# Clipped relative attention on one core: 64-row turns placed beside the scores, 64-column projections placed beside the values, and some copies moved between engines

## The reference

```python
q, k, v = split_heads(x @ Wq.T), split_heads(x @ Wk.T), split_heads(x @ Wv.T)   # 16 heads of 64
sim = einsum('bid,bjd->bij', q, k) * scale
idx = clip(r[None, :] - r[:, None], -16, 16) + 16
sim = sim + einsum('btd,tsd->bts', q, rel_k_table[idx]) * scale
attn = softmax(sim)
out = einsum('bij,bjd->bid', attn, v) + einsum('bts,tsd->btd', attn, rel_v_table[idx])
out = merge_heads(out) @ Wo.T + bo
```

## Time and profile before

| | |
|---|---|
| median of 3 runs | 2304.55 us (2299.51 to 2312.35) |
| profiled execution, own time | 2308.97 us |
| its span | 2307.3 us |
| TensorE busy / weight loads | 2030.2 us (88%) / 1226.8 us |
| VectorE, ScalarE, GpSimd busy | 1536.3, 1136.8, 746.6 us |
| mean granted TensorE clock | 0.955 |
| the stage that is changed | scores from 1605.1 to 2155.0 us of the span |

### The profile page before, as it was taken

One profiled execution on the slowest core, in us unless ns is written; L12 is line 12 of the kernel. 1 busy time (PEld: TensorE's weight loads), 2 busy tenths in 40 slices (PEclk: granted clock), 3 DMA queues, 4 the chain that ended last, 5 costly groups with the idle time before them and its releaser, 6 DMA issues.

```text
span 2307.3 us, 40672 instructions
## 1 busy us (share of the span) xinstructions
PE 2030.2 (88%) x15704; PEld 1226.8 (53%) x15704; DVE 1536.3 (67%) x3079; ACT 1136.8 (49%) x1854; POOL 746.6 (32%) x1057
## 2 busy tenths in 40 slices
PE   5886789988868989998998898998999999999888
PEld 2342466666644455445564344445666666666546
DVE  5685678888678777755556774024877777777663
ACT  2575456656614454563332566223664655646442
POOL 4544434333037847441002331002223232232133
PEclk7998899999979999999998999999999999999999
DMA  4430111111323524202002320001664564645252
GB/s 139 127 100 2 29 29 29 33 24 29 97 86 118 152 67 141 70 16 102 1 1 64 106 71 2 31 1 56 182 184 147 157 184 132 185 148 157 80 112 55
DMA packets 183975, 198.87 MB, mean 86 GB/s; under 512 B 55922, under 2 KB 152486, under 8 KB 179302
## 3 DMA queue, kind: packets, MB, share of 16 engines
q1 hardware_dynamic: 183782, 196.27, 28.9%
HBM read 93.53 MB, written 92.08 MB: 80 GB/s over the span
## 4 chain that ended last, share of the span: by engine, by line
PE 34%; DVE 10%; ACT 4%; DMA 3%; issue 2%; SPq 1%; POOL 1%; DVEq 0%; ACTq 0%; POOLq 0%
PE PS L2097 5%; DVE AR L2411 4%; PE PS L1950 3%; PE PS L2326 3%; PE PS L2333 2%; PE PS L1937 2%; PE PS L1940 2%; DMA RA<-ZP 2%; PE PS L2295 2%; PE PS L2348 2%; PE PS L2675 1%; ACT AR L2491 1%; DVE PS L2408 1%; PE PS L597 1%; PE PS L2365 1%
## 5 line engine op out<-in xcount | busy, mean ns | idle before, releaser
L2491 ACT ACTIVATE AR<-PS,AR 128x512 f32<-128x512 f32 x256 | 173.6, 686 | 181.1 <-DVE AR L2411 181.0
L1275 ACT ACTIVATE AR<-PS 128x1024 f32<-128x1024 f32 x160 | 162.6, 1024 | 124.4 <-PE PS L1024 123.5
L2537 POOL TENSOR_TENSOR RA<-AR,RA 128x288 f32<-128x288 f32 x128 | 88.0, 698 | 374.6 <-ACT AR L2491 190.1
L718 ACT ACTIVATE AR<-PS 128x1024 f32<-128x1024 f32 x160 | 162.8, 1024 | 94.1 <-PE PS L576 46.4
L1128 DVE TENSOR_REDUCE AR<-PS 128x2 f32<-128x768 f32 (+1 forms) x192 | 159.9, 864 | 56.1 <-PE PS L1004 29.5
L2411 DVE TENSOR_REDUCE AR<-PS 128x2 f32<-128x1024 f32 x128 | 156.7, 1224 | 9.0 <-DVE PS L2408 0.5
L2333 PE MATMUL PS<-CC,AR 128*128 128x128 f32 x1024 | 140.0, 280 | 20.1 <-DVE AR L2417 16.0
L2333 PEld LDWEIGHTS PS<-CC,AR 128*128 128x128 f32 x1024 | 110.3, 141 | 72.3 <-issue 37.7
L2326 PE MATMUL PS<-AR 64*128 64x200 f32 (+2 forms) x1280 | 131.4, 349 | 3.0 <-ACT AR L2491 3.0
L1821 POOL TENSOR_TENSOR AR<-AR 128x1024 f32<-128x1024 f32 x32 | 75.5, 2358 | 174.9 <-DVE AR L1669 174.9
L2326 PEld LDWEIGHTS PS<-AR 64*128 64x128 f32 x1280 | 103.8, 188 | 39.4 <-issue 29.8
(11 more groups left out here) (367 smaller groups left out, 4978.2 us busy)
## 6 DMA issues: line engine op xcount, KB each, us to landing
ZD<-RC SPq DMA_DIRECT2D x32, 1152.0 KB
AR<-ZD SPq DMA_DIRECT2D x32, 640.0 KB
ZP<-AR SPq DMA_DIRECT2D x128, 160.0 KB, 2.6
SP<-AR SPq DMA_DIRECT2D x40, 384.0 KB, 2.6
AR<-SP SPq DMA_DIRECT2D x128, 96.0 KB
RA<-SP SPq DMA_DIRECT2D x32, 384.0 KB
SP<-AR SPq DMA_DIRECT2D x40, 256.0 KB, 2.9
RC<-RC SPq DMA_DIRECT2D x64, 130.0 KB
```

Of the source, the lines that this page charges most:

```text
L718: e.activation(self.PT[m % 6], C.PS[:, 2 * s:2 * s + 2, :], ACT.Exp).then_inc(S["s_turned"].sem, 1)
L1275: e.activation(self.PT[m % 6], C.PS[:, 2 * s:2 * s + 2, :], ACT.Exp).then_inc(S["s_turned"].sem, 1)
L2491: i = e.activation(self.PP[n % 5][:, hh, 16:528], C.bank[2 * (n % 2) + hh], ACT.Exp, bias=self.NMX[n % 4][:, hh:hh + 1], accum_out=self.DE ...
L2537: e.tensor_tensor(self.XM[:, 2 * q:2 * q + 2, :], self.PP[n % 5][:, :, 128 * q:128 * q + 144], W["edge"].unsqueeze(1).broadcast_to((128, 2 ...
```

## The change

It does five things, all in the stage `Clipped`.

1. A block's turns are cut in the two halves of the array's rows. Queries 0 to 63 of both heads are turned in rows 0 to 63 and go to one bank of the ring, queries 64 to 127 in rows 64 to 127 and go to another. There are 16 turns of 64 x 128 instead of 8 of 128 x 128, issued alternately for the two halves, and both banks have to be free before the first of them. The same is done with `wt`.
2. The full products (`q`, `k`, `vals`, `rel`, `close`, `wo`) are each issued as two products of 64 columns of the array (`columns`).
3. The order of a half becomes: turns of a block four earlier, scores, turns, scores, `wt`; and then `av`, `q`, `k`, `rel`, `close`, `vals`, `wo`. The turns move from two blocks behind to four, `av` from six and five to eight and seven, and the list has one more half at its end.
4. Copies move: of the 256 turned banks VectorE now copies 64 and ScalarE 192 (before 160 and 96). The second copy of the keys is made by GpSimd, from the first and a difference of biases. The small table copies of `qr` go to GpSimd, ahead of its broad ones.
5. The copies write into the turned probabilities with a stride, 8 pieces of 64, and that of `wt` is two copies of 4 x 64 instead of one of 512.

```diff
+def columns(e, o, x, y, **how):
+    for g in range(0, 128, 64):
+        i = e.matmul(o[g:g + 64], x[:, g:g + 64], y, **how)
+    return i
...
-            if n < N:
-                plan.extend([("scores", n), ("scores", n + 1)])
-            plan.extend(("av", m) for m in (n - 6, n - 5) if 0 <= m < N)
...
+            for m in (n, n + 1):
+                if 0 <= m - 4 < N:
+                    plan.extend([("backs" if m % 2 else "backv", m - 4, 0), ("backs", m - 4, 1)])
+                if m < N:
+                    plan.append(("scores", m))
             if n < N:
+                plan.extend([("exp", n), ("band", n)])
+            if first and 0 <= p - 2 < 32:
+                plan.extend([("wt", p - 2, 0), ("wt", p - 2, 1), ("send", p - 2)])
+            if n < N:
+                plan.extend([("exp", n + 1), ("band", n + 1)])
+            plan.extend(("av", m) for m in (n - 8, n - 7) if 0 <= m < N)
...
-            e.matmul(o, wq, C.XT[:, p // 8, 0:512], start=True, stop=True).then_inc(S["t_" + kind].sem, 1)
+            columns(e, o, wq, C.XT[:, p // 8, 0:512], start=True, stop=True).then_inc(S["t_" + kind].sem, 1)
...
-            for k in range(4):
-                i = e.transpose(o[:, 128 * k:128 * k + 128], self.PP[n % 5][:, hh, 16 + 128 * k:144 + 128 * k], C.ident)
-            i.then_inc(S["t_" + kind].sem, 1)
+            if g == 1:
+                w.wait_ge(S["s_exp"], n)
+                one = "backs" if n % 2 else "backv"
+                both = C.bank[(4, 5, 7)[self.ring.slot[one, n, 0]]], o
+                for a in range(8):
+                    for x in range(2):
+                        h = slice(64 * x, 64 * x + 64)
+                        i = e.transpose(both[x][:, 64 * a:64 * a + 64], self.PP[n % 5][h, a // 4, 16 + 128 * (a % 4):144 + 128 * (a % 4)], C.ident[h, h])
+                        if a == 7:
+                            i.then_inc(S["t_backs" if x else "t_" + one].sem, 1)
...
-            e.activation(self.K0[p % 2], o, ACT.Identity, bias=W["rk0"])
-            e.activation(self.K32[p % 2], o, ACT.Identity, bias=W["rk32"]).then_inc(S["s_k"].sem, 1)
+            e.activation(self.K0[p % 2], o, ACT.Identity, bias=W["rk0"]).then_inc(S["s_k"].sem, 1)
...
+            e.tensor_copy(CP[:, 0:4, 127:159], self.RE[:, 0:4, p % 2, :])
+            e.tensor_copy(CP[:, 4:8, 128:160], self.RE[:, 4:8, p % 2, :]).then_inc(S["g_qr"].sem, 1)
...
+            e.tensor_scalar(self.K32[p % 2], self.K0[p % 2], self.DK, None, ALU.add).then_inc(S["g_k"].sem, 1)
```

More of the change, by code:

```diff
@@ L2203, in __init__ @@
                   "wo": 1, "turnx": 1, "turn": 1, "table": 1},
-            "v": {"init": 2, "qr": 1, "vals": 1, "scores": 2, "backv": 1, "xsum": 1, "sums": 2, "close": 1, "wo": 1, "fin": 5},
+            "v": {"init": 2, "vals": 1, "scores": 2, "backv": 1, "xsum": 1, "sums": 2, "close": 1, "wo": 1, "fin": 5},
             "s": {"turn": 1, "table": 1, "q": 1, "k": 1, "rel": 1, "exp": 1, "backs": 1, "wt": 1, "fin": 1, "turnx": 1},
-            "g": {"init": 1, "qr": 1, "vals": 1, "band": 1, "wo": 1},
+            "g": {"init": 1, "qr": 2, "k": 1, "vals": 1, "band": 1, "wo": 1},
         }
@@ L2227, in order @@
         plan.extend(("vals", 0, k, hf) for k in range(NT) for hf in range(2))
-        for n in range(0, N + 12, 2):
+        for n in range(0, N + 14, 2):
             p, first = n // 4, n % 4 == 0
@@ L2260, in order @@
                     plan.append(("rel", p // 2 + 1))
+                if 0 <= p - 2 < 32:
+                    plan.append(("close", p - 2))
                 if 0 <= p - 1 < 32:
-                    plan.extend([("wt", p - 1), ("send", p - 1)])
+                    plan.append(("sums", p - 1))
             m = n - 32
-            if m >= 0 and m % 32 in (2, 4) and n < N:
-                plan.extend(("vals", m // 32 + 1, m % 32 - 2 + i, hf) for i in range(2) for hf in range(2))
-            b, m = (n - 38) // 32, (n - 38) % 32
+            if m >= 0 and m % 32 in (4, 6) and n < N:
+                plan.extend(("vals", m // 32 + 1, m % 32 - 4 + i, hf) for i in range(2) for hf in range(2))
+            b, m = (n - 40) // 32, (n - 40) % 32
             if 0 <= b < NB:
@@ L2273, in order, with turned @@
                     plan.append(("turnx", b))
-            if first and 0 <= p - 2 < 32:
-                plan.append(("close", p - 2))
-        return plan
+        return plan
+    def turned(self, n, g):
+        rows = self.PT[n // 4 % 2].rearrange("p (q h) (k x j) -> p q (h k) x j", q=4, k=4, x=2)
+        return rows[:, n % 4, :, g, :]
     def span(self, q):
@@ L2320, in on_tensor @@
             w.wait_ge(S["s_q"], p)
[L2321 removed]
+            w.wait_ge(S["g_k"], p)
             w.wait_ge(S["s_exp"], n - 2)
@@ L2351, in on_tensor @@
         elif kind == "wt":
-            p, = key
-            w.wait_ge(S["v_sums"], p)
-            for q in range(NT):
-                i = e.transpose(o[:, 128 * q:128 * q + 128], self.WT[p % 2][:, 2 * q:2 * q + 2, :].rearrange("p h e -> p (h e)"), C.ident)
-            i.then_inc(S["t_wt"].sem, 1)
+            p, g = key
+            if g == 1:
+                w.wait_ge(S["v_sums"], p)
+                both = C.bank[(4, 5, 7)[self.ring.slot["wt", p, 0]]], o
+                for q in range(NT):
+                    for x in range(2):
+                        h = slice(64 * x, 64 * x + 64)
+                        i = e.transpose(both[x][:, 64 * q:64 * q + 64], self.WT[p % 2][h, 2 * q:2 * q + 2, :].rearrange("p h e -> p (h e)"), C.ident[h, h])
+                        if q == 3:
+                            i.then_inc(S["t_wt"].sem, 1)
         elif kind == "close":
             p, = key
-            w.wait_ge(S["s_wt"], p)
-            e.matmul(C.bank[6], W["rvb"], self.WX, start=False, stop=True).then_inc(S["t_close"].sem, 1)
+            w.wait_ge(S["s_wt"], p, 1)
+            columns(e, C.bank[6], W["rvb"], self.WX, start=False, stop=True).then_inc(S["t_close"].sem, 1)
         elif kind == "wo":
@@ L2412, in on_vector @@
         elif kind == "backv":
-            n, hh = key
+            n, g = key
             if n % 4 == 0:
```

66 lines of the change are left out of this document (29 added, 37 removed).

## The result

The changed kernel takes 2264.95 us, the median of 4 runs (2264.10 to 2269.71); the kernel before takes 2305.17 beside it, the median of 4. The ratio is 0.9827, with a 95% interval of 0.9804 to 0.9850: 40 us less, where 62 were forecast. The measured time lies inside the range of 2207 to 2288.

A forecast was written before the change was run, and what follows sets the result against it. The stage was taken as bound by TensorE, with about 1 us a head pair from the ring's three banks. Savings of 2.11 us times 32 head pairs, 67.5, less 5.5, gave 62 saved: 2244 us, range 2207 to 2288.

The forecast's parts named there:

- the main term: TensorE's turns: 16 pairs at 0.061 us take 0.98 instead of 1.72 in each half, saving 1.48 us a head pair.
- Rivals 1: TensorE's turns: a pair goes at the pace of its loads, 0.107 us, so turns save nothing; 2296 us, chance 0.07.
- 4 (0.2): TensorE's turns: a pair's two loads do not overlap, so it takes 0.2 us; slower, about 2400 us, chance 0.05.
- `wt`: The turns of `wt` on TensorE: from 0.43 to 0.24 us, saving 0.19 a head pair.
- The switches: Changes of the array's division on TensorE: two instead of three a half, 0.22 us each, saving 0.44 a head pair.
- The waits: TensorE's waiting in a head pair: 1.1 us afterwards, as much as before, so the sum of savings stands.
- My walk: One head pair followed through the new order across the engines: 13.6 us on average, 1.1 of it waiting.
- Rival 2: Waits at the query's copy and the bank behind `close` grow, losing 1 us more a head pair; 2276 us, chance 0.12.
- its sign, over 2 us idle a head pair: TensorE's idle time before the turns: over 2 us a head pair would show that the waits had grown.
- Rival 3: Copies ahead of the maxima cut the loop and most of the 1.1 us waiting vanishes; 2214 us, chance 0.10.
- The ends: One more half in the list, TensorE draining behind VectorE's and ScalarE's copies with two ring banks: +4 us.
- The copies: Work a head pair: VectorE 12.6 to 10.6 us, ScalarE 9.6 to 10.6; GpSimd's key copy 0.7; all under TensorE's 12.4.

The follow-up runs named there:

- run with scores together: The changed kernel with a half's row part ordered turns, scores, scores, turns instead of turns, scores, turns, scores: 2270.08 us, ratio 0.9856.
- run with both moves: The changed kernel with the query's product and copy between the two blocks' exponentials and VectorE's sums ahead of the scaling of `close`: 2248.12 us, ratio 0.9753.
- sums first alone: The changed kernel with VectorE's sums of a half moved ahead of its scaling of `close`, nothing else moved: 2260.91 us, ratio 0.9816.
- the query's move: The changed kernel with the query's product and copy moved between the exponentials of the first half's two blocks: 2255.34 us, ratio 0.9794.

## Why the prediction was right and where it was wrong

**The direction and the main term.** Turns were to bring 1.48 us a head pair. A block's 16 instructions stand 0.52 us ahead of the next group (1944.02 to 1944.54). Their record is 0.71 long and that of a single one 0.23, so the other 15 follow at 0.032 us, a pair in 0.063, where 0.061 was taken. So 16 pairs take 1.01 in place of 1.72, 0.71 in each half and 1.42 a head pair. The run with full turns shows that the gain hangs on this term: without it 45 us are lost, some of them to the switches that full turns bring in these places. Rivals 1 (a pair at 0.107) and 4 (0.2) are refuted: with them the eight pairs would take 0.86 or 1.6 us.

The load of a turn takes 140 ns in 64 rows, as in 128, and yet a pair goes in 0.063. The Trainium skill (TensorE: Matmul & The Clock Gate, "LDWEIGHTS (loading the stationary operand)") has a load of 128 columns occupy 107 ns whatever its rows, by an estimate from its rule. For turns in two row halves this case's trace disagrees: two such loads go by in 0.063 us.

**`wt`** was to bring 0.19. It takes 0.37 us to the start of `av`, the switch included (1939.76 to 1940.13), where it took 0.53: 0.16.

**The switches: the step that failed in the work.** I took a half's rest of 0.66 us for three changes of division, 0.22 each, and struck one out. In the changed kernel the half without waits takes 5.85 us; its moving takes 1.01 for turns, 1.71 for scores, 1.71 for `av` and 0.85 for `close`, 5.28. So 0.57 is left for two changes: only 0.09 of the 0.22 was saved, 0.18 a head pair in place of 0.44, 8 us in all. The run with column halves undone confirms that a change is worth its 0.20; the run with scores together shows what came in its place: turns and scores that alternate cost about 0.16 for the further meeting, though both are in row halves. I had counted changes of division and not changes between turns and products.

These terms make 1.42 + 0.16 + 0.18 = 1.76 a head pair where 2.11 was forecast, so 56.3 us, or 54.8 less the 1.5 for the first head pairs. From the first scores to the end TensorE's busy time fell by 58.6 - 4.4 = 54.2, where 66 were forecast: 11.8 us are missing here. The agreement is good to a few us only, since busy time also holds the shortest waits, such as the 0.14 that the prediction read inside a group.

**The waits: the other step that failed.** I wrote that the waits stay as they were, 1.1 us a head pair. They rose by 12.2 us in the stage. Both numbers of the step were off in the head pairs that it walked through: there the idle time was 0.5 a head pair before (8.0 in sixteen) and is 0.7 now (11.1; 0.61 in most). My walk came to the mean of 13.6 only because it gave `rel`, which stands in every other head pair, 0.45 us where it takes 0.87 (1934.44 to 1935.31), while it had the wait for the query too long, 0.5 for 0.22; the one for the bank, 0.35 for 0.39, came near. With `rel` right it gives 13.8, near the 14.04 measured in this part (28.07 for the two head pairs from 1921.80). And it walked through ordinary head pairs alone: three quarters of the added waiting, 9.1 us, lie at the start and around the changes of batch, which it did not look at.

Rival 2 named the two places rightly, the copy of the query and the bank behind `close`, and each has its wait; but as they replace the old one, they add 3 us and not 32, and its sign, over 2 us idle a head pair, did not come in the ordinary head pairs. Rival 3 (the waits go) did not hold as the change stands. The run with both moves shows that it could be had in the ordinary head pairs: 2.6 us of idle are left in sixteen.

**The ends.** Behind the last scores 5.8 us came, of which 1.4 are waiting; 4 were forecast. Together 11.8 (work) + 12.2 + 1.4 (waiting) - 4 (forecast for the ends) are the 21 us between the 62 forecast and the 41 that stage and end show (46.4 - 5.8).

**The copies.** GpSimd's copy of the keys was sized wrongly (1.57 for 0.7) and is hidden, as the run without it shows. VectorE's and ScalarE's work came near: 10.28 and 10.35 us in the head pair (ScalarE 11.48 where `rel` stands), 10.6 each forecast. That the shares of the copies matter by their place in VectorE's queue, by 19 to 24 us, I had not said; I counted only their sum.

**The column halves** bring about 5 us as the kernel stands (the intervals overlap, the traces show 0.2 a head pair), where the 0.44 a head pair made 14. At the measured 0.20 a half they would be worth 13 (64 halves) if nothing waited; in the first halves the wait for the query covers it.

**Left open.** Why sums first alone brought 4 us where 13 were expected, and 7 more beside the query's move (2248.12 against 2255.34). Which step in the head pairs around a change of batch makes TensorE wait longer than before. And the small copies of `qr` on GpSimd, which no run takes back alone.

## What to carry to other kernels

When work in the bounding engine shrinks, follow the buffers it fills: a bank that is refilled right after it was filled cost its whole turn-round here, whichever engine copied, so a shorter operation and its new place have to be tried together; alone, the new place brought nothing here and the shorter operation cost 20 us. Afterwards read the two or three waits that return in every round and look at what stands ahead of their releaser in its queue: two moves in the order gave 17 us more, with no work taken away. Split a change in the idle time by place before naming its cause: a total of 12 us fitted the two waits of the ordinary rounds, and three quarters of it lay elsewhere. In a forecast by walking through the order, check the walk first on the kernel before, piece by piece, until it gives the measured round, and walk through the rounds that differ from the others too.

## What the runs showed of the hardware

- Turns of 64 x 64 fp32, two row halves side by side, follow one another every 31 to 32 ns, with weight loads of 140 ns each; turns in all 128 rows start 109 ns apart.
- Turns and products that alternate within one division of the array cost about 0.16 us for a further meeting, in the one comparison made; a change of division cost 0.20.
- With half turns in the old order a PSUM bank was free again for TensorE 1.49 to 1.66 us after the first of 0.5 us of turns into it, of which the copy is 0.5 to 0.6 (1.90 once, where `rel` stands).
- A copy of 128 x 512 fp32 values that writes 8 pieces of 64 took no longer than one that writes them in one piece: 0.67 against 0.68 to 0.69 us on VectorE, 0.60 both on ScalarE.
- On GpSimd adding a column to 128 x 512 fp32 values took 1.57 us, longer than adding two such tiles, 1.27.
- The granted clock in the stage stayed at 0.99 to 1.00, the level of 2.4 GHz, though 1,984 of its 5,429 TensorE instructions are turns of 64 columns.
